# A routing table written by 64 indirect transfers of GpSimd instead of built by matrix products

## The reference, cut to what matters

```python
scores = jax.nn.softmax(xt @ Wg.T, axis=-1)                     # xt: 2048 x 512, E = 16
group_scores = scores.reshape(T, G, E // G).max(axis=-1)        # G = 4 groups, 2 are kept
topi = jax.lax.top_k(masked, TOPK)[1]                           # TOPK = 4 experts of a token
combine = zeros((T, E)).at[arange(T)[:, None], topi].add(weights)
h = silu(einsum('td,eid->eti', xt, W1)) * einsum('td,eid->eti', xt, W3)
y = einsum('etd,te->td', einsum('eti,edi->etd', h, W2), combine)
z = silu(xt @ Ws1.T) * (xt @ Ws3.T) @ Ws2.T
x = x + tanh(g_ffn[0]) * (y + z)
```

## Time and profile before

| | |
|---|---|
| median of 3 runs | 1238.58 us (1228.62, 1238.58, 1242.21) |
| the profiled execution | 1229.68 us, its span 1227.9 us |
| granted TensorE clock, mean | 0.985 |
| PE busy | 1190.7 us, 97% of the span |
| PEld, DVE, ACT, POOL busy | 917.2, 631.8, 576.0, 618.1 us |
| all 16 DMA engines together | 128 GB/s on average |

### The profile page before, as it was taken

The page is one execution under the profiler, slowest core; times in us unless marked ns, Lnnn a source line. Parts: engine busy times, 40 slices in busy tenths (PEclk is TensorE's granted clock), DMA queues, the critical chain, the costliest instruction groups (busy, mean ns, idle before and its releaser), DMA issues. The chain is left out here.

```text
span 1227.9 us, 23555 instructions
## 1 busy us (share of the span) xinstructions
PE 1190.7 (97%) x7779; PEld 917.2 (75%) x7780; DVE 631.8 (51%) x1829; ACT 576.0 (47%) x989; POOL 618.1 (50%) x655
## 2 busy tenths in 40 slices
PE   7999999999988989999998999999999999999996
PEld 5564555555543468888887999999999999999995
DVE  5437999999947847865141233222423344442100
ACT  1221777777741333322332555555555555555553
POOL 5010333443332615635562766667666676666663
PEclk8999999999989989999999999999999999999998
DMA  9462544444449250110133546566565655656433
GB/s 351 150 192 99 155 127 124 133 128 129 147 132 256 85 206 32 38 38 32 52 123 114 116 101 146 142 147 146 147 144 122 169 146 147 147 147 144 73 69 43
DMA packets 74829, 157.73 MB, mean 128 GB/s; under 512 B 10836, under 2 KB 16468, under 8 KB 73608
## 3 DMA queue, kind: packets, MB, share of 16 engines
q1 hardware_dynamic: 53720, 106.96, 27.1%
q0 software_dynamic: 21040, 49.88, 19.8%
HBM read 101.88 MB, written 52.49 MB: 126 GB/s over the span
## 5 line engine op out<-in xcount | busy, mean ns | idle before, releaser
L1555 DVE CAST e_w<-e_w 128x480 fp32r<-128x480 f32 x135 | 71.5, 530 | 304.9 <-DMA e_w<-in_w2T 300.8
L670 DVE CUSTOM_DVE_ANT_0 a_mb<-a_mb,late 128x512 f32<-128x512 f32 (+1 forms) x480 | 217.3, 526 | 6.4 <-PE a_mb L712 4.6
L1711 PE MATMUL e_yps<-e_w,e_hT 128*128 x711 | 197.2, 404 | 0.9 <-ACT e_hT L1620 0.9
L656 ACT ACTIVATE a_at<-a_eb 128x1024 f32<-128x1024 f32 (+1 forms) x192 | 163.5, 870 | 38.3 <-PE a_eb L733 25.7
L1582 POOL DMA_INDIRECT out<-e_y,scatter x79 | 130.4, 1651 | 99.0 <-ACT e_y L1629 95.4
L576 POOL TENSOR_SCALAR_AFFINE_SELECT a_at<-a_at 128x256 f32<-128x256 f32 (+1 forms) x192 | 93.8, 489 | 171.0 <-ACT a_at L656 170.9
L1690 PE MATMUL e_up<-e_w,e_xT 128*128 x948 | 170.5, 329 | 0.0
L1690 PE MATMUL e_gate<-e_w,e_xT 128*128 x948 | 168.8, 327 | 1.0 <-issue 1.0
L1690 PEld LDWEIGHTS e_gate<-e_w,e_xT 128*128 128x128 f32 x948 | 156.8, 190 | 11.1 <-issue 6.3
L1690 PEld LDWEIGHTS e_up<-e_w,e_xT 128*128 128x128 f32 x948 | 149.7, 189 | 0.0
L1711 PEld LDWEIGHTS e_yps<-e_w,e_hT 128*128 128x128 f32 x711 | 128.1, 189 | 25.4 <-issue 1.2
(11 more groups left out here) (259 smaller groups left out, 1858.3 us busy)
## 6 DMA issues: line engine op xcount, KB each, us to landing
e_w<-in_w13T SPq DMA_DIRECT2D x16, 1408.0 KB, 7.1
dq<-p_parts SPq DMA_DIRECT2D x32, 256.0 KB, 2.4
a_q<-dq SPq DMA_DIRECT2D x64, 128.0 KB
do<-a_o SPq DMA_DIRECT2D x32, 256.0 KB, 2.3
e_w<-in_w2T SPq DMA_DIRECT2D x16, 512.0 KB, 4.2
a_k<-dk SPq DMA_DIRECT2D x64, 98.0 KB
e_w<-in_ctxT SPq DMA_DIRECT2D x4, 1024.0 KB, 15.3
e_w<-in_x SPq DMA_DIRECT2D x4, 1024.0 KB, 13.7
```

What stands on the lines that cost most here:

```text
L656: eng.activation(to, scores, ACT.Exp, scale=0.25).then_inc(s_exp, 1)
L670: eng.tensor_tensor_reduce(out=b[:, 0:w], in0=b[:, 0:w], in1=io["late"][:, SEQ - w:SEQ], scale=1.0, scalar=3 * NEG, op0=ALU.add, op1=ALU.m ...
L1711: mm = eng.matmul(yps[:], hT[r][0:size, mine, n, :], w[0:size, bass.ds(buf, 1), its * SIDE + at:its * SIDE + at + D].rearrange("p b n -> p ...
```

## The change

PE no longer builds the table, and DVE no longer makes the matrices for it. Instead the table is an array `dtable` in DRAM of 10112 rows (one for each slot) with 2 words of 4 bytes, token and scale.

- POOL writes a blank table to SBUF at the start of the stage (an iota and a memset in place of two iotas), and SP copies it to `dtable`.
- DVE computes `place`, the row of `dtable` for each pair (a multiplication, an addition and a cast on 128 x 64), where before came the products' matrices.
- POOL issues 64 indirect transfers, each of which writes 128 rows of 8 bytes, one from each partition, to the rows that `place` names (function `enter`). Their places: 3 behind `raw` of each of the first five units of batches 1 and 2, 13 behind `raw` of the sixth, and 2 behind `raw` of each of units 18 to 21.
- In batches 1 and 2 (`listed`) DVE takes over from POOL the subtraction for `h` (12 times), the low part of `xT` (twice) and the sums (8 times; DVE reads `yps` itself, so ACT's scaling of these blocks falls away as well). PE then waits for DVE's sum instead of ACT's `part` before it reuses `yps` (`freed`).
- In the last batch SP waits for all 64 transfers, reads the table back to SBUF, and only then goes on to the loads of expert 0's weights, which have stood at this place before. DVE waits for the table and makes `scatter`, `gather` and `scale` of it by three instructions.
- The first 4 gathers stand ahead of unit 23 instead of unit 20.

```diff
-            for t in range(NT):
-                r = t % 2
-                if t >= 2:
-                    eng.wait_ge(s_tok, t)
-                eng.tensor_tensor(at_row[r], iota_p[:].rearrange("p (o n) -> p o n", o=1).broadcast_to([P, NK, P]),
...
+            eng.tensor_scalar(row[:], row[:], float(TILES), None, ALU.mult).then_inc(s_v, 1)
+            eng.wait_ge(s_v, next(done))
+            eng.tensor_tensor(row[:], row[:], col[:], ALU.add).then_inc(s_v, 1)
+            eng.wait_ge(s_v, next(done))
+            eng.tensor_copy(place[:], row[:]).then_inc(s_v, 1)
...
+            for b in listed:
+                for i in range(b * NS, (b + 1) * NS):
...
+                    eng.wait_ge(s_hhigh, i + 2)
+                    eng.tensor_tensor(h[0:size, 1, n, :], raw[i % 2][0:size], h[0:size, 0, n, :].bitcast(F32), ALU.subtract).then_inc(s_hlow, 1)
+                for j in range(CH):
...
+                    eng.wait_ge(s_down, i + 2)
+                    eng.scalar_tensor_tensor(out=x1[b][:, j, :], in0=yps[i % 2][:], scalar=tg[:, 0:1], in1=x1[b][:, j, :],
+                                             op0=ALU.mult, op1=ALU.add).then_inc(s_sum, 1)
+                    if j == 0:
+                        eng.wait_ge(s_xhigh, b + 2)
+                        eng.tensor_tensor(xT[:, 1], xT[:, 1].bitcast(F32), xT[:, 0].bitcast(F32), ALU.subtract).then_inc(s_xlow, 1)
+
+            eng.wait_ge(s_table, 16)
+            eng.tensor_copy(io["scatter"], index).then_inc(s_v, 1)
...
+            def enter(count):
+
+                for t, k in itertools.islice(entries, count):
+                    eng.indirect_dma_start(out=dram["table"], out_offset=bass.IndirectOffsetOnAxis(ap=place[:, t, k:k + 1], axis=0),
+                                           in_=put[:, t, k, :], in_offset=None).then_inc(s_entry, 16)
...
-                if i == (BATCH - 1) * NS + 2:
+                if i == NS:
+                    eng.wait_ge(s_blank, 16)
+                    eng.wait_ge(s_v, placed[0])
+                if i == (BATCH - 1) * NS + 5:
                     eng.wait_ge(s_v, compared[1])
...
+                if b in listed:
+                    enter(3 if n != order[-1] else 13)
+                    continue
+                if b == BATCH - 1:
+                    enter(2)
...
-                if NS + 2 <= i < NS + 2 + NT // 2:
-                    for t in range(2 * (i - NS - 2), 2 * (i - NS - 2) + 2):
-                        table(t)
...
                 if b == BATCH - 1:
+                    eng.wait_ge(s_entry, 16 * NT * NK)
+                    eng.dma_start(table[:], dram["table"].rearrange("(p g) w -> p g w", p=P)).then_inc(s_table, 16)
                     eng.wait_ge(io["s_base"], 16 * CH * b)
                     eng.wait_ge(s_v, compared[0])
                     load_first(eng, io, 0, 0)
```

More of the change, by code:

```diff
@@ L1243, in _ @@
             eng.wait_ge(s_v, next(done))
-            eng.tensor_tensor(put[:, :, :, 0], rows(tok[:].rearrange("p (t o) -> p t o", o=1), NK), row[:], ALU.subtract).then_inc(s_v, 1)
+            eng.tensor_scalar(row[:], row[:], float(TILES), None, ALU.mult).then_inc(s_v, 1)
             eng.wait_ge(s_v, next(done))
-            for t in range(NT):
-                r = t % 2
-                if t >= 2:
-                    eng.wait_ge(s_tok, t)
-                eng.tensor_tensor(at_row[r], iota_p[:].rearrange("p (o n) -> p o n", o=1).broadcast_to([P, NK, P]),
[L1251 to L1259, removed]
+            eng.tensor_tensor(row[:], row[:], col[:], ALU.add).then_inc(s_v, 1)
+            eng.wait_ge(s_v, next(done))
+            eng.tensor_copy(place[:], row[:]).then_inc(s_v, 1)
+            placed.append(next(done))
+            eng.wait_ge(s_v, placed[0])
             eng.wait_ge(io["s_xTout"][BATCH - 2], 32)
@@ L1282, in _ @@
             eng.wait_ge(s_v, next(done))
-            eng.wait_ge(s_tok, NT + 1)
-            eng.tensor_scalar(indexf[:], tokps[:, 0:TILES], pad[:, 0:1], None, ALU.add).then_inc(s_v, 1)
-            eng.wait_ge(s_v, next(done))
[L1286 to L1290, removed]
+            for b in listed:
+                for i in range(b * NS, (b + 1) * NS):
+                    n = units[i][1]
+                    size = SCH[n][1]
+                    if i == listed[0] * NS:
+                        eng.wait_ge(s_hlow, i + 1)
+                    eng.wait_ge(s_hhigh, i + 2)
+                    eng.tensor_tensor(h[0:size, 1, n, :], raw[i % 2][0:size], h[0:size, 0, n, :].bitcast(F32), ALU.subtract).then_inc(s_hlow, 1)
+                for j in range(CH):
+                    i = b * CH + j
+                    if i == listed[0] * CH:
+                        eng.wait_ge(s_sum, i + 1)
+                    eng.wait_ge(s_down, i + 2)
[6 more added lines that the diff above has]
+            eng.tensor_copy(io["scatter"], index).then_inc(s_v, 1)
+            eng.wait_ge(s_v, next(done))
+            eng.tensor_scalar(io["gather"], index, T - 1, None, ALU.min).then_inc(s_v, 1)
             compared.append(next(done))
             eng.wait_ge(s_v, compared[1])
-            eng.tensor_copy(io["scale"], tokps[:, TILES:]).then_inc(s_v, 1)
+            eng.tensor_copy(io["scale"], table[:, :, 1]).then_inc(s_v, 1)
             eng.wait_ge(s_v, next(done))
@@ L1345, in _ @@
                     for j in range(CH):
-                        if b * CH + j < NT - 1:
+                        if b not in listed and b * CH + j < NT - 1:
                             result(b, j)
@@ L1389, in _ @@
         def _(eng):
[L1390 removed]
+            begin(eng, s_mm, s_gate, s_up, s_down)
             PASSES = ((0, 0), (0, 1), (1, 0))
@@ L1421, in down @@
                     mm.then_inc(s_down, 1)
-            def table(t):
-                r = t % 2
-                eng.wait_ge(s_row, 3 * t + 4)
-                for k in range(NK):
-                    mm = eng.matmul(tokps[:], at_row[r][:, k, :], at_col[r][:, k].rearrange("p n g -> p (n g)"), start=t == 0 and k == 0,
-                                    stop=t == NT - 1 and k == NK - 1, skip_group_check=True)
-                mm.then_inc(s_tok, 1)
             for i, (b, n) in enumerate(units):
```

58 lines of the change are left out of this document (33 added, 25 removed).

## The result

The changed kernel took 1214.85 us in the median of four runs (1213.87 to 1216.92), the kernel before 1233.6 us in four runs beside it (1227.48 to 1242.21): a ratio of 0.9856, with an interval of 0.9812 to 0.99. Six further executions of the same changed kernel, beside 17 of the kernel before (1231.32 us), gave 1218.54 us and 0.9897 (0.9863 to 0.993). It is faster, by 12.8 us in the larger sample; the median of the first four lies 2.2 us under the predicted range, whose low end was 1217.

What follows compares the result with a forecast made beforehand. PE was taken to bound the kernel everywhere. Products gone (-17.4), stall (0) and tail (+3.8) sum to -13.6 us, which from the median 1238.6 gives 1225.0 us, range 1217 to 1252.

Steps and rivals of the forecast that it cites:

- Products gone, -17.4: PE in batches 1 and 2: eight groups of table products at 2.18 us leave its path, 17.4 us gained.
- The price, 1.31: POOL's time per indirect transfer, p, taken as 1.31 us from the last two of four gathers in a row.
- no stall at it: PE in batches 1 and 2: stall of 0 at p = 1.31, and zero up to p = 1.40.
- PE's patience: Unit 20's raw product started some 3.8 us late behind four gathers, yet PE kept its pitch of 5.44 us.
- The formula 56p - 78.6: PE's stall in us over batches 1 and 2, for a price of p us a transfer.
- the rivals' prices: POOL per transfer: 1.9 us, total 1256 us, chance 0.17; or 1.45 to 1.65 us, 1227 to 1239 us, chance 0.15.
- Landing, 3.3 us after the issue: Last batch: the last transfer lands 3.3 us after its issuing ends, at 622.4; bounds 2.0 and 4.5 us.
- the lower bound of the earlier trace: Low bound for the last transfer's landing: 2.0 us, a direct store's whole time.
- Stall of the last low part, 2.0: Last batch: the low part comes at 633.7, PE wants it at 631.7, a stall of 2.0 us.
- Splits, 12.0 us: DVE's nine splits of the weights at the stage's end take 12.0 us, with some three POOL products beside them.
- The late tail, +3.8: Stage end: late weights make the splits end at 644.9, 3.8 us after the unhindered down products' end at 641.1.
- The level: The difference of -13.6 us was taken from the three runs' median, 1238.6, 8.9 us above the profiled execution's 1229.68.

Runs made afterwards that it cites:

- e6: Changed kernel with 12 more indirect transfers in batch 0, plain or accumulating, of 8 to 2048 bytes a row; 1228.72 us in one execution.
- e5b: Changed kernel with every fourth transfer issued twice, the copy to a second table, 80 in all; 1236.18 us, ratio 1.0044 to the kernel before.
- e5: Changed kernel with every second transfer issued twice, the copy to a second table, 96 in all; 1261.37 us, ratio 1.0272 to the kernel before.
- e2: Changed kernel with SP's loads of expert 0's weights moved ahead of its wait for the transfers; 1217.4 us, ratio 0.9878 to the kernel before.
- e3: Changed kernel with weights' loads ahead of SP's wait and the four gathers behind the last unit's low part; 1213.41 us, again 1217.66 us.
- e9: As e3, with DVE also taking the last batch's sums of blocks 1 and 2; 1212.01 us, ratio 0.9856 to the kernel before.
- e8: Changed kernel with DVE's 128x2048 subtraction for xT's low part cut into four of 128x512; 1219.06 us in one execution.

## Why the prediction was right or wrong

**Products gone, -17.4: right.** -17.25 in the stretches, +16.7 when they were put back.

**The price, 1.31, and no stall at it: right.** 1.26 measured; PE's busy share in both batches is over 0.99. That there is none up to 1.40 was not tested. PE's patience, read as some 3.8 us from the earlier trace rows, is 3.6 (unit 20's raw product at 630.82, where unit 23's at 643.50 less three pitches of 5.44 gives 627.18); no term used it. The choice of the plain gather over the accumulating scatter was right for the reason given, as e6 shows. The four gathers of the changed kernel, with DVE idle beside them, took 1.01, 0.97, 0.95 and 0.95 us, so the 1.24 and 1.46 of the first two before were indeed disturbed ones; but the other two, at 0.99 and 0.96, had casts beside them as well. The formula 56p - 78.6 was near beyond its zero in the two batches that it counts (11.6 for 10.4, 24.7 for 27.8) and left out what the backlog costs in the last batch, 6.6 and 12.6 (e5b, e5). It changed only the rivals' prices, not the forecast.

**Landing, 3.3 us after the issue: wrong term.** It took 1.15 until SP's next issue, from the issue's start 2.1 us. The row it came from was that of an accumulating scatter of 2 KB rows, whose addition made it dear already when issued; the lower bound of the earlier trace rows, a direct store's 2.0 from issue, would have been near. Even that bound was set too high, since the prediction counted the 2.0 from the end of issuing, and the earlier trace rows counts from the issue. The Trainium skill (DMA: Bandwidth & Descriptors, section "Anatomy of one DMA — SWDGE (gpsimd) path") puts the fixed cost at about 2.0 us; the trace agrees, with 2.1.

**Stall of the last low part, 2.0: mis-sized.** 0.68, as SP was 2.1 us earlier than forecast, counted from the same head.

**Splits, 12.0 us: mis-sized.** 14.2, nearly the 15.25 of before. The gathers were through before the splits began, but five instructions of POOL ran beside them, the last product, the low part and three sums, where the prediction counted some three: the cast at 638.04, beside the sum at 637.81, took 1.51 us, where quiet ones took 0.40. With the earlier start they still ended 1.1 us ahead of the forecast, counted from the same head.

**The late tail, +3.8, put down to the splits: near in size by luck, wrong in cause.** Measured from batch 3 on: 0.95 + 3.1 + 0.5 = 4.6. An earlier landing, longer splits and a path that the sum did not have happened to come near 3.8. The splits made DVE's last sum start at 642.23, 1.3 us later than 0.2 after PE's end; POOL's path then held the stage for 1.4 more (645.40 against 642.97 + 1.06); the way from POOL's memset to the first gate product, 3.3 us before, took 3.8, with the transposes at 1.09 us for 0.63. No term of the prediction had POOL's path at the end of a stage, and e2 shows that taking the splits' lateness away alone returns 0.2 us of PE's idle time.

**The level: the step that failed.** The sum against the profiled execution gave 1216.1 us, and that execution took 1215.58. The prediction then took the difference from the median of three runs, 1238.6, and so added 8.9 us which belonged to those executions, not to the kernel. 17, 5 and 9 further executions of the kernel before gave medians of 1231.32, 1228.46 and 1230.18 us, near the profiled one's 1229.68. Of the 10.2 us between the forecast 1225.0 and the measured 1214.85, this step is 8.9; 0.5 is the sum's and 0.7 the distance of the profiled execution from its median. With the level of the profiled execution the range 1217 to 1252 becomes 1208 to 1243 and holds the measured time. That the sum met the profiled execution within 0.5 us is partly luck: 1.5 of its 14.1 us lie ahead of batch 1, where nothing was changed, and from there on it is 12.6 for the forecast 13.6.

What varies between executions lies for the most part ahead of batch 1: it began at 498.43 and 506.55 us in two profiles of one and the same kernel (e3), whose `stage_shared` had begun at 452.21 and 458.31, while from batch 1 on they took 711.2 and 711.7. What in the earlier stages varies was not examined.

## What to carry to other kernels

Moving small scattered writes from TensorE's products to indirect stores pays when GpSimd's round, here 1.26 us a transfer and its own arithmetic, stays under TensorE's; give its arithmetic away together with it. In this kernel an issued transfer is paid twice on GpSimd, when it is issued and once more, 0.08 us, where the stage ends, so let GpSimd's last work of such a stage be early. And with executions that differ by 1%, predict from the execution whose profile was read, and give the median's distance to it to the range, not to the number.

## What the runs showed of the hardware

- At the end of `stage_shared` GpSimd stood idle the longer, the more indirect stores the stage had issued, also when the added ones lay in batch 0 (48: 4.81 us, with DVE's path as good as tied, 64: 6.12, 76: 7.09, 80: 7.42, 96: 8.73), 0.082 us for each. The 0.9 us that the line leaves for none is an estimate, near the 1.06 us from DVE's last sum to the next stage. What GpSimd does in that time no view shows.
- An indirect store of 128 rows took 0.96 us for rows of 8 bytes and 0.97 to 1.10 for rows of 512 and 2048, with 0.30 to the next, and 1.54 to 1.76 when it accumulated (8 and 512 bytes).
- A transfer issued beside DVE's 128x2048 subtraction of two SBUF inputs took up to 2.87 us. The Trainium skill (SBUF — State Buffer, section "Who interferes with whom") has such an instruction contend with GpSimd's reads, and by this the trace agrees; the same section infers that it does not hold up a transfer's descriptor generation. These indirect transfers were held up, and were under 1.2 us with the narrow subtractions; whether it is the reading of their index or the descriptors that waits, no row shows.
- TensorE's products of a batch took 50 instead of 45.8 us at a granted clock of 0.85 to 0.87, in batches in which it had waited up to 10.6 us at a time. The four transposes behind its idle time took 1.09 us at a granted clock of 0.50 (after 4.03 us) and 0.63 us at 1.00 (e9, after 1.35 us), the lower and the higher of its levels, 1.2 and 2.4 GHz. The length of the idle time does not settle it: in e8 they took 0.63 us after 4.02 us, at a granted clock of 0.97:

```profile
649.29 0.63 PE L1698 MATMUL e_xps<-ident,e_x 128*128 128x128 f32 x4 [4.02 <-POOL e_h L1614]
```
